# A Toeplitz tile built in quarters under its convolution, and bias loads moved from ScalarE to GpSimd

## The reference

```python
y = jax.lax.conv_general_dilated(x, w, window_strides=(1,), padding=[(K - 1, 0)],
        feature_group_count=D, dimension_numbers=('NWC', 'WIO', 'NWC'))
x = x + (y + b)                       # w = cond_2048[:, None, :], K = 128 rows
def cell(h, x):
    gi = x @ W_ih + b_ih
    gh = h @ W_hh + b_hh
    i_r, i_z, i_n = jnp.split(gi, 3, axis=-1)
    h_r, h_z, h_n = jnp.split(gh, 3, axis=-1)
    r = jax.nn.sigmoid(i_r + h_r)
    z = jax.nn.sigmoid(i_z + h_z)
    n = jnp.tanh(i_n + r * h_n)
    h_new = (1.0 - z) * n + z * h
    return (h_new, h_new)
_, hs = jax.lax.scan(cell, cond_2048, jnp.swapaxes(x, 0, 1))
out = x + jnp.swapaxes(hs, 0, 1)
```

## Time and profile before

| | |
|---|---|
| median of 3 runs | 1207.98 us (1207.88 to 1209.65) |
| the profiled execution | 1208.6 us, span 1207.0 us |
| PE busy | 1172.4 us, 97% |
| VectorE, ScalarE, GpSimd busy | 537.6, 500.6, 295.4 us |
| PE's first early convolution instruction | 30.38 us |
| first product of step 1 | 75.46 us |

### The profile page before, as it was taken

How to read it: one execution, slowest core, us unless ns; L and a number is a source line. 1 busy time by engine, 2 the same in 40 slices (tenths; PEclk the granted TensorE clock), 3 DMA queues, 4 the chain that set the end, 5 groups by cost and what they waited for, 6 DMA issues and landing times.

```text
span 1207.0 us, 15341 instructions
## 1 busy us (share of the span) xinstructions
PE 1172.4 (97%) x5518; PEld 981.1 (81%) x5518; DVE 537.6 (45%) x811; ACT 500.6 (41%) x934; POOL 295.4 (24%) x527
## 2 busy tenths in 40 slices
PE   1999999999999999999999999999999999999997
PEld 1988888888888888888888888888888888888885
DVE  2746766767663343333433334343333433334333
ACT  3547777777763233332333233332333323333231
POOL 0341121211203222222222222222222222222211
PEclk9999999999999999999999999999999999999999
DMA  9998899889732101111011110111111111011100
GB/s 245 286 227 174 193 205 187 183 184 191 185 97 70 30 26 33 35 35 28 25 34 35 35 27 25 35 35 35 26 26 35 35 35 26 26 35 35 35 18 18
DMA packets 231458, 97.98 MB, mean 81 GB/s; under 512 B 212752, under 2 KB 217360, under 8 KB 229376
## 3 DMA queue, kind: packets, MB, share of 16 engines
q1 hardware_dynamic: 210816, 62.96, 24.1%
q0 software_dynamic: 16256, 33.32, 10.2%
q10 hardware_dynamic: 4352, 1.25, 0.4%
HBM read 63.34 MB, written 34.14 MB: 81 GB/s over the span
## 4 chain that ended last, share of the span: by engine, by line
PE 96%; DMA 1%; ACT 1%; ACTq 1%; issue 0%; DVE 0%; POOL 0%; SPq 0%; POOLq 0%; DVEq 0%
PE bank L787 86%; PE bank L809 5%; PE bank L749 2%; PE bank L776 2%; DMA early<-early_result 1%; ACT toep_early L508 0%; ACTq L484 0%; DMA tap_pad<-tap_rows 0%; DMA xT<-early 0%; DMA h<-in_cond_dram 0%; POOL out_dram L440 0%; POOL xT L425 0%; PE bank L760 0%; ACTq L489 0%; ACT L586 0%
## 5 line engine op out<-in xcount | busy, mean ns | idle before, releaser
L440 POOL DMA_DIRECT2D out_dram<-outZ x256 | 140.2, 550 | 795.9 <-DVE outZ L738 775.2
L787 PE MATMUL bank<-w_ih_hi,xT_hi 128*128 128x512 f32 x768 | 305.9, 398 | 0.3 <-ACT bank L527 0.3
L787 PE MATMUL bank<-w_ih_lo,xT_hi 128*128 128x512 f32 x768 | 299.9, 390 | 0.0
L787 PE MATMUL bank<-w_ih_hi,xT_lo 128*128 128x512 f32 x768 | 299.9, 390 | 0.0
L787 PE MATMUL bank<-w_hh_hi,hT_hi 128*128 128x512 f32 x768 | 299.6, 390 | 0.0
L787 PE MATMUL bank<-w_hh_lo,hT_hi 128*128 128x512 f32 x768 | 299.5, 390 | 0.0
L787 PE MATMUL bank<-w_hh_hi,hT_lo 128*128 128x512 f32 x768 | 298.8, 389 | 0.0
L787 PEld LDWEIGHTS bank<-w_ih_hi,xT_lo 128*128 128x128 f32 x768 | 144.2, 188 | 31.3
L787 PEld LDWEIGHTS bank<-w_hh_hi,hT_lo 128*128 128x128 f32 x768 | 144.2, 188 | 30.5
L787 PEld LDWEIGHTS bank<-w_hh_hi,hT_hi 128*128 128x128 f32 x768 | 144.4, 188 | 28.1
L787 PEld LDWEIGHTS bank<-w_hh_lo,hT_hi 128*128 128x128 f32 x768 | 144.4, 188 | 27.5
(11 more groups left out here) (62 smaller groups left out, 988.6 us busy)
## 6 DMA issues: line engine op xcount, KB each, us to landing
x_unit<-in_x_dram SPq DMA_DIRECT2D x64, 256.0 KB, 5.1
toep_ring<-kernel_parts SPq DMA_DIRECT2D x128, 128.0 KB, 3.5
out_dram<-outZ POOLq DMA_DIRECT2D x256, 64.0 KB, 1.9
xres<-stage SPq DMA_DIRECT2D x32, 384.0 KB, 5.1
xT<-xres POOLq DMA_DIRECT2D x192, 64.0 KB, 2.1
early<-early_result SPq DMA_DIRECT2D x4, 1024.0 KB, 13.5
xT<-early POOLq DMA_DIRECT2D x60, 64.0 KB, 3.4
w_ih_raw<-in_L_cond_W_ih_dram SPq DMA_DIRECT2D x12, 256.0 KB, 7.4
```

The source lines that it names most:

```text
L440: pool.dma_start(out[:, bass.ds(t, 1), :].rearrange("(Q s) o (q e) -> q s Q (o e)", s=QUAD, e=P)[q4], outZ[u % 2][q4 * QUAD:(q4 + 1) * QUA ...
L787: mm = nc.tensor.matmul(psum[:, :], a[:, rows], b[w][:, cols], start=False, stop=stop and n == 2, skip_group_check=True)
```

## The change

Three things change. ScalarE's seven loads of the convolution's bias (conv_b_rows, bias_d, bias_pair) are issued by GpSimd, behind its first memsets and ahead of its wait for the GRU's biases; the one semaphore of bias_d and bias_pair becomes two. The multiplications that build toep_early go over a quarter of the channels at a time, and of the eight blocks ScalarE makes three and VectorE five; ScalarE makes y0 behind its first quarter. PE waits for a quarter ahead of the first matmul that reads it, and for y0 only ahead of the first bank that is bank 7.

```diff
+        ACT_BLOCKS = 3
+        def toep_early_block(c, n):
+            gs = slice(n * G0 // QUARTERS, (n + 1) * G0 // QUARTERS)
+            return toep_early[:, :].rearrange("p (g q u h) -> p q h u g", g=G0, q=QUADS, u=EARLY)[:, c // 2, c % 2, :, gs]
+        def tap_quarter(n):
+            gs = slice(n * G0 // QUARTERS, (n + 1) * G0 // QUARTERS)
+            return tap_blocks[:, :].rearrange("p (u g) -> p u g", g=G0)[:, :, gs]
...
+            pool.dma_start(conv_b_rows[:, :], conv_b.rearrange("(c g) -> c g", g=G0)).then_inc(conv_b_rows_loaded, 16)
+            for q4 in range(QUADS):
+                pool.dma_start(bias_d[q4 * QUAD:(q4 + 1) * QUAD, :],
...
+                               allow_slow_non_contiguous=True).then_inc(bias_d_loaded, 16)
+            for c in range(2):
...
+                pool.dma_start(bias_pair[c * T:(c + 1) * T, :].rearrange("s (n g) -> s n g", g=UNIT),
...
+                               ).then_inc(bias_pair_loaded, 16)
             pool.wait_ge(bias_loaded, 16 * 4)
...
-            act.dma_start(conv_b_rows[:, :], conv_b.rearrange("(c g) -> c g", g=G0)).then_inc(conv_b_rows_loaded, 16)
...
-            for q4 in range(QUADS):
-                act.dma_start(bias_d[q4 * QUAD:(q4 + 1) * QUAD, :],
...
-            for c in range(2):
...
-                act.dma_start(bias_pair[c * T:(c + 1) * T, :].rearrange("s (n g) -> s n g", g=UNIT),
...
-            for c in range(C0 // 2):
-                nc.scalar.activation(toep_early_block(c), tap_blocks[:, :].rearrange("p (u g) -> p u g", g=G0),
-                                     ACT.Identity, scale=in_block[:, c:c + 1]).then_inc(toep_early_ready, 1)
-            act.wait_ge(conv_bias_loaded, 16 * (QUADS + 2))
-            act.wait_ge(x_row_done, 1)
-            for k in range(KB):
...
+            for n in range(QUARTERS):
+                for c in range(ACT_BLOCKS):
+                    nc.scalar.activation(toep_early_block(c, n), tap_quarter(n),
+                                         ACT.Identity, scale=in_block[:, c:c + 1]).then_inc(toep_early_ready, 1)
+                if n == 0:
+                    act.wait_ge(bias_d_loaded, 16 * QUADS)
+                    act.wait_ge(x_row_done, 1)
+                    for k in range(KB):
...
+            act.wait_ge(bias_pair_loaded, 16 * 2)
             high_weights(1)
...
+            for n in range(QUARTERS):
+                for c in range(ACT_BLOCKS, C0):
+                    nc.vector.tensor_scalar(toep_early_block(c, n), tap_quarter(n),
+                                            in_block[:, c:c + 1], None, ALU.mult).then_inc(toep_early_dve_ready, 1)
...
-            pe.wait_ge(toep_early_ready, C0 // 2)
-            pe.wait_ge(toep_early_dve_ready, C0 // 2)
             pe.wait_ge(x_early_loaded, 16 * 4)
-            pe.wait_ge(y0_ready, KB)
             for g in range(G0):
                 n, slot = g * B // BANK, g * B % BANK
+                if g % (G0 // QUARTERS) == 0:
+                    quarters = g * QUARTERS // G0 + 1
+                    pe.wait_ge(toep_early_ready, ACT_BLOCKS * quarters)
+                    pe.wait_ge(toep_early_dve_ready, (C0 - ACT_BLOCKS) * quarters)
+                if slot == 0 and conv_bank[n % 3] is ps_x0 and n < 3:
+                    pe.wait_ge(y0_ready, KB)
```

More of the change, by code:

```diff
@@ L183, in conv_residual_gru @@
         bias_loaded = sem("bias_loaded")
-        conv_bias_loaded = sem("conv_bias_loaded")
+        bias_d_loaded = sem("bias_d_loaded")
+        bias_pair_loaded = sem("bias_pair_loaded")
         bias_rz_ready = sem("bias_rz_ready")
@@ L409, in _ @@
                              0.0).then_inc(k_zeroed, 1)
+            pool.dma_start(conv_b_rows[:, :], conv_b.rearrange("(c g) -> c g", g=G0)).then_inc(conv_b_rows_loaded, 16)
+            for q4 in range(QUADS):
+                pool.dma_start(bias_d[q4 * QUAD:(q4 + 1) * QUAD, :],
+                               conv_b[q4 * P:(q4 + 1) * P].rearrange("(k r) -> r k", r=QUAD),
+                               allow_slow_non_contiguous=True).then_inc(bias_d_loaded, 16)
+            for c in range(2):
+                first = conv_b[c * UNIT:(c + 1) * UNIT]
+                pool.dma_start(bias_pair[c * T:(c + 1) * T, :].rearrange("s (n g) -> s n g", g=UNIT),
+                               bass.AP(first.tensor, first.offset, [[0, T], [2 * UNIT, NUNIT], [1, UNIT]])
+                               ).then_inc(bias_pair_loaded, 16)
             pool.wait_ge(bias_loaded, 16 * 4)
@@ L506, in _ @@
             act.wait_ge(in_block_set, 1)
-            for c in range(C0 // 2):
-                nc.scalar.activation(toep_early_block(c), tap_blocks[:, :].rearrange("p (u g) -> p u g", g=G0),
-                                     ACT.Identity, scale=in_block[:, c:c + 1]).then_inc(toep_early_ready, 1)
-            act.wait_ge(conv_bias_loaded, 16 * (QUADS + 2))
-            act.wait_ge(x_row_done, 1)
-            for k in range(KB):
-                nc.scalar.activation(xT[0][:, k * P:(k + 1) * P], ps_x0[:, k * P:(k + 1) * P], ACT.Identity,
-                                     bias=bias_d[:, k:k + 1],
-                                     scale=k_full[:, k * P + T - 1:k * P + T]).then_inc(y0_ready, 1)
+            for n in range(QUARTERS):
[6 more added lines that the diff above has]
+                    for k in range(KB):
+                        nc.scalar.activation(xT[0][:, k * P:(k + 1) * P], ps_x0[:, k * P:(k + 1) * P], ACT.Identity,
+                                             bias=bias_d[:, k:k + 1],
+                                             scale=k_full[:, k * P + T - 1:k * P + T]).then_inc(y0_ready, 1)
             act.wait_ge(y0_ready, KB)
@@ L547, in _ @@
             act.wait_ge(k_parts_stored, 16 * QUADS)
-            act.wait_ge(toep_early_ready, C0 // 2)
-            act.wait_ge(toep_early_dve_ready, C0 // 2)
+            act.wait_ge(toep_early_ready, ACT_BLOCKS * QUARTERS)
+            act.wait_ge(toep_early_dve_ready, (C0 - ACT_BLOCKS) * QUARTERS)
+            act.wait_ge(bias_pair_loaded, 16 * 2)
             high_weights(1)
@@ L647, in _ @@
             dve.wait_ge(in_block_set, 1)
-            for c in range(C0 // 2, C0):
-                nc.vector.tensor_scalar(toep_early_block(c), tap_blocks[:, :].rearrange("p (u g) -> p u g", g=G0),
-                                        in_block[:, c:c + 1], None, ALU.mult).then_inc(toep_early_dve_ready, 1)
+            for n in range(QUARTERS):
+                for c in range(ACT_BLOCKS, C0):
+                    nc.vector.tensor_scalar(toep_early_block(c, n), tap_quarter(n),
+                                            in_block[:, c:c + 1], None, ALU.mult).then_inc(toep_early_dve_ready, 1)
             low_part(xT_lo, xT[0], xT_hi, xT_hi_ready, xT_lo_ready, 1)
```

7 lines of the change are left out of this document (removed).

## The result

The changed kernel takes 1211.89 us (median of nine runs, 1210.54 to 1215.58), beside 1209.29 us of the kernel before in nine runs on the same chip (1207.88 to 1210.88): a ratio of 1.0027, with a 95% interval of 1.0016 to 1.0039 (the two medians alone give 1.0021). It is slower by some 2.6 us, where 1209.5 and "no difference" were forecast.

A forecast was written before the change was run, and what follows sets the result against it. The prediction took the DMA queue, through the last store's landing at 66.3 us, to bound the start of step 1. Terms 0, -0.2 and +1.7 put it 1.5 above the median 1207.98: 1209.5 us, range 1206.9 to 1211.4 (8 in 10).

The forecast's parts named there:

- What bounds the kernel: Ahead of step 1: the DMA queue sets the last store's landing at 66.3 us, not the convolution; PE released at 75.46.
- The train: The four early_result stores land one behind another after w_hh (56.73 us), 2.43 us each, whatever their time of issue.
- ScalarE's stream and the start of the convolution: Start of kernel: ScalarE's work moves up 6.1 us; convolution waits for x_early, starting at 22.8, 7.6 us earlier.
- The stall of up to 3.5 us: Early convolution: evictions behind VectorE's weight splits could hold PE some 3.5 us at the fifth bank; end between 51.2 and 54.7.
- Landing 66.3, gain 0: Early-result stores: issued earlier but behind the w_hh loads in a full queue, so the last lands at 66.3 as before; term 0.
- The moved loads, -0.2: Seven bias loads on GpSimd: issue covered by its wait, engine time 0, and -0.2 us from filling an early hole; bounds 0.9 either way.
- The read-back and release: After the last store: xT lands at 72.1 and PE is released for step 1 at 75.46, both as before.
- The restart, 1.7 us (0 to 1.7): Step 1's first products: PE, idle 7.9 us, restarts at half clock and loses 1.7 us, with 0 at the other end.
- rival B: Same store train, but no loss at PE's restart, or PE late anyway: 1207.8 us, 1206.9 to 1208.4; chance 0.24.
- The base: Median of the kernel before, taken as 1207.98 us; the profiled execution was put 0.6 above it.
- C: Slower: PE's clock stays at 1.2 GHz after 75.46 for more than 12 matmuls; 1210.4 to 1211.8 likelier; chance 0.18.
- D: Faster: last store follows its convolution, not throughput, so all 7.6 us come off: 1200.4, or 1203.9 with a stall; chance 0.12.

The follow-up runs named there:

- rows_after: Changed kernel with the four broadcast loads of the GRU's biases (1.57 MB) replaced by two 6 KB rows spread by matmuls; 1206.80 us, ratio 0.9978.
- less_dma: Changed kernel without the load of bias_tmp (0.5 MB), so b_hh is left out of the biases of r and z; 1210.80 us, ratio 1.0006.
- again: The changed kernel run once more, unedited, for a second profile; 1211.95 us, ratio to before 1.0019.
- late_again: Changed kernel with the kernel_parts stores issued after the first four w_ih_hi, run a second time for a second trace; 1212.01 us, ratio 1.0016.
- pair_late: Changed kernel with bias_pair issued by ScalarE behind tap_blocks and kernel_parts stores issued after the first high part of w_ih; 1209.93 us, ratio 1.0005.
- pair_act: Changed kernel with the two bias_pair loads issued by ScalarE behind tap_blocks, conv_b_rows and bias_d staying on GpSimd; 1210.19 us, ratio 1.0003.
- loads_only: Kernel before with only the seven bias loads moved from ScalarE to GpSimd; 1209.75 us, ratio 1.0002.
- each part alone: Two kernels: quarters with the seven loads kept on ScalarE, 1209.30 us; the kernel before with only the seven loads moved to GpSimd, 1209.75 us.
- warm: Changed kernel plus 30 matmuls nobody reads, on PE between the end of step 0 and the wait for step 1; 1209.49 us, ratio 1.0005.
- small_act: Changed kernel with conv_b_rows and bias_d issued by ScalarE and only bias_pair by GpSimd; 1211.55 us, ratio 1.0012.

## Why the prediction was wrong

- **What bounds the kernel: right.** The chain goes through the last store, the read-back, ScalarE's table load and r, and the put of r's bias releases PE. rows_after moves the end by taking bytes away, and less_dma's landing goes the same way; 7.6 us of PE's start brought no gain. The train is right too: the last store lands 9.6 us after the last piece of w_hh before and after (4 x 2.4 in the prediction).
- **ScalarE's stream and the start of the convolution: right.** 22.8 was predicted, with x_early as last wait; it is 22.79, and the row names x_early. The first block is at 15.84 (15.4 predicted). The blocks had ended by 23.5 (24.5 predicted). But kernel_parts was issued at 18.86 already, 11.4 us earlier than before, and the prediction didn't ask what these stores would meet: they fell among x_early's packets.
- **The stall of up to 3.5 us: right in kind, smaller.** It is 1.91 us, since w_ih_hi began at 29.95 and not at 32.1. The convolution ends at 53.3, between the two figures given (51.2 and 54.7). PE ended step 0 at 69.66, not at 67.5.
- **"Landing 66.3, gain 0": the step that failed.** The last store was issued at 56.16, not 52: VectorE's weight splits stand between its evictions and wait for ScalarE's w_hh_hi, which stands behind ScalarE's puts of the biases, GpSimd's sum of them (45.57) and the landing of bias_hn (45.50). This part would have cost nothing. But it landed at 68.38 (again: 68.28), 2.0 us later than before. The argument was that the bytes ahead of the store are the same, so the landing is the same. In its place the runs showed that the order and the queue of issue move the loads ahead at equal bytes: the last piece of w_hh was there at 58.77 instead of 56.73, and the stores followed it at the same distance. bias_pair on GpSimd beside the quarters is worth 1.6 us of landing (late_again against pair_late), the earlier kernel_parts 0.9 to 1.4 us (pair_act against pair_late, again against late_again). The mechanism by which bias_pair does it stays open; a hole in the engines' share (0.51 at 17 to 19 us) goes with it, but loads_only has one too and lands early. The same argument missed the other way as well: each part alone lands 1.3 us earlier. x_unit was taken as unchanged by the same reasoning, from a memset at 60.24; the memset came at 62.41. The step had no bounds in the sum, and the range none for it.
- **The moved loads, -0.2 (bounds 0.9 either way): the wrong quantity was costed.** Their engine time did fall, from 1.8% of 66.4 us (1.2 us, where the count of packets had given 1.9) to 1.0%, by some 0.5 us. But bias_pair on GpSimd together with the quarters costs about 2 us (late_again against pair_late), outside the bounds of 0.9. The bounds were for what the descriptors take of the engines, not for when other transfers get through.
- **The read-back and release: right within 0.5 us.** From landing to release 9.62 us, against 9.12 before; again 8.65. On the profiled executions the terms are then +2.0 for the landing, +0.5 here and +2.7 for the restart, together the 5.2 us of span; the prediction had 0, 0 and 1.7.
- **The restart, 1.7 us (0 to 1.7): mechanism right, size too small.** It cost 2.72 and 2.51 us (8.44 and 8.23 less 5.72), and warm gives 2.46 us of median back. The upper bound was worked out from the 3.5 us of work ahead of the convolution; in the restart the slow products run for 5.7 us (78.00 to 83.7). The doubt whether the convolution hides the clock is answered by the windows above: 11 instructions in 2 us at a clock of 0.56 and 11 at 1.00. Its row was no evidence for rival B.
- **The base.** The median of three runs, 1207.98, was low: 9 to 35 runs of before in each group give 1209.16 to 1209.69. The sum of +1.5 on 1209.3 would have been 1210.8. That explains 1.3 us of the 2.4 by which the forecast fell short; the landing and the restart are the rest. The profiled execution of before had 1208.6, and the prediction read it as late when it was early.
- **Rivals.** C came closest in time (1210.4 to 1211.8), with the clock low for 13 of 24 products where it asked for more than 12. That it comes so near is luck: its restart is 1.0 us more than the forecast's, and the rest of the distance is the landing and the low base, which it didn't have. D is excluded: with the convolution over 5.5 us earlier the store landed later. No rival had the store land later than before for the order of issue; C only added 0.9 us for dear descriptors, and those turned out cheaper. It was the missing one.

## What to carry to other kernels

Where a queue of transfers sets the end of a stage, an earlier producer shows up as idle time of its consumer, and on TensorE that idle time can have a price of its own: here 2.5 us of restart, which matmuls that nobody reads took away. Reordering issues at unchanged bytes made this full queue later by 2.0 us and, with either half of the reordering, earlier by 1.3, so such a step wants a bound on both sides and not a zero; taking 1.57 MB out ahead of it gave the changed kernel some 5 us. To find what made the last transfer late, look for the last row that is late by the same amount: here the loads of w_hh, not the stores. And three runs didn't fix the base to 0.1%.

## What the runs showed of the hardware

- An fp32 convolution of 128x128 matmuls, each with its own weights, keeps its pace at 1.2 and at 2.4 GHz: 11 instructions in 2 us in both windows above. Products of 128x512 take 0.43 and 0.23 us. In the trace of before the clock column reads 1.00 beside four products 0.43 apart: it doesn't show every slow stretch.
- The same issue on GpSimd's queue, bias_pair with 512 runs of 128 bytes, takes 0.71 us in one place and 5.06 in another, with 4.16 us between the two in which GpSimd has no record; on ScalarE's the two took 1.38 us before and 3.30 us in pair_act. What sets an issue's time wasn't tested.
- The first 24 products after an idle time took 5.72 us after 0.73 and 5.73 after 2.26 us of it, and 7.05 to 8.50 us after 3.97 to 8.45 us, with the slowest behind one of the shortest of these (small_act, 4.27 us).
